# Order of the opening's weight loads, ScalarE's rounding of two weights, one weight scaled a batch earlier, and idle matrix products in three stretches

## The chip, the core and the metric

The kernel runs on one core of one Trainium2 chip. The metric is the time of one execution on the device in microseconds (us), as the median of several runs. The engines are TensorE (PE, matrix products), VectorE (DVE), ScalarE (ACT), GpSimd (POOL) and SyncE (SP, which here only issues transfers). TensorE's clock is granted at one of two levels, 2.4 GHz (shown as 1.00) and 1.2 GHz (0.50).

## What is computed

Two transformer layers over a batch of B = 32 items with T = 112 rows of D = 256 numbers, and a context of S = 375 rows for each item. All in float32, with four blocks in a row:

```
x = x + cross_attention_0(layernorm(x), ctx)     # 16 heads of 64, Wq Wk Wv: 256 -> 1024, Wo back, + bo
x = x + ffn_0(layernorm(x))                      # rows quantised to 8 bits, weights to -1, 0, 1; depthwise conv of 3 taps, silu
x = x + cross_attention_1(layernorm(x), ctx)     # 16 heads of 16, rms norm of q and k, rotation
x = x + ffn_1(layernorm(x))                      # one uint8 scale for ALL activations, int8 scale per weight row, relu
```

The weights of ffn_0 are quantised as `clip(round(w * scale), -1, 1)` with `scale = 1 / clip(mean(|w|), 1e-5)`. The weights of ffn_1 are quantised row by row: `scale = max(|w|) / 127`, `round(w / scale)`. The activations of ffn_1 share one scale, `max(x) / 255`, over the whole batch, so ffn_1 can begin only when all 32 items have passed the third block; its hidden layer has a second such scale.

## The kernel before, in words

Each engine runs a program of its own, written out by hand; the engines meet only at semaphores (`wait_ge`, `then_inc`). There is no planner: the order of the lines is the order on each engine. A helper `link` makes a DVE instruction wait for the one before it.

**Precision.** A product that has to be near exact is made from split operands: `hi` is the operand rounded to the format `F32R`, `lo` is what is left, and three products hi·lo, lo·hi and hi·hi are summed (`exact3`, six matmuls since the depth is 2 x 128). ACT makes `hi` by a copy, DVE makes `lo` of a weight by a subtraction, POOL makes `lo` of the context (`ctx_lo`, L1493 to 1496).

**Opening** (L262 to 301 on SP, L647 to 671 on PE, L917 to 933 on ACT, L1297 to 1341 on DVE, L1561 to 1566 on POOL). SP loads ident, the first context (`craw`), the first x, wk0 into `stage[0]`, wv0 into `stage[1]`, eight small constants and wq0. `stage` has two rooms of 128 x 2048 numbers, and each next weight waits until its room is free: wkv1 after wk0's lo (semaphore `w_lo` 1), f0w1 after wv0's lo, f0w2 after wkv1's lo, and wo0 after f0w1 is quantised (`w_quant` 1). DVE clears some tiles and marks that with `zeros_ready`. ACT rounds wk0, then the context; DVE and POOL subtract. PE then makes the keys of item 0 (`k0_proj`, eight pieces), the values (`v0_proj`, six), the queries (`q0_proj`, two), and goes into the attention. DVE makes the ternary weights in `ternary(n, part)` (L1098 to 1116): a sum of absolute values (part 0), mean and reciprocal behind PE's product with ones (`weight_sum`, part 1), then four passes over 2048 numbers (parts 2 to 4: scale and clip above, clip below and add ROUND, subtract and clip, clip and cast). For f0w1 these stand before the attention of the opening, for f0w2 inside it, at i = 2, 4 and 6.

**Attention** (`attention(part, b)` on PE L496, ACT L819, DVE L1135, POOL L1502) works through pairs of heads, i = 0 to 7 in the opening and in the closing, 0 to 15 in a middle batch, where layer 0 of the next item and layer 1 of this one are mixed. A pair goes: scores (PE, L410), maxima (DVE, L1048), two exps (ACT, L808), reciprocal of the sums (DVE, L1056), scaling (POOL, L1508), turning (PE, L434 or L424), copies of the turned rows (half by ACT, L768, half by DVE, L1039 or L1035), products with the values (PE, L446 for layer 0, L461 for layer 1). Scores run two pairs ahead. PE's turn of pair i waits for ACT's and DVE's copies of pair i - 1. Behind the last pairs stand the keys and values of layer 1 (`kv1_proj`), which DVE squares and sums (`k1_squares`) and POOL rotates, and the product with Wo (`wo0_product`), whose second half and the residual belong to the next batch.

**Loop.** For b = 0 to 30 every engine runs `rest(b, False)` and `attention(MIDDLE, b)`. `rest` finishes layer 0 of item b (residual x1, quantisation xq, ffn_0 with its convolution, x2) and the query of layer 1, and PE fills its waits with the projections of item b + 1.

**Last batch** (L616 to 639 and the branches with `last_batch`). `rest(31, True)` has no next item, so the fills fall away. DVE there also prepares the weights of ffn_1: `scales(0, 0)` (largest of each row, L1177 to 1180), `scales(0, 1)` (division, L1182) and `scales(0, 2)` (rounding, L1185) stand between `oT_lo` and x1 (L1194 to 1200), `scales(1, 0)` ahead of x2 (L1257), `scales(1, 1)` behind it. `attention(CLOSING, 31)` follows.

**Tail** (PE L680 to 762). The weights are turned, the global scale is found with two small products (L692 and L694, `spread`), the hidden layer is made once for its maximum (`hidden`, L701, with `largest` on DVE, L1412), a second `spread` follows (L726, L728), then the hidden layer is made again (`hidden_again`), passed through ACT's relu (L986), rounded by DVE and multiplied with the second weight (`second`, L743); POOL adds the residual (L1582, L1587) and SP stores.

## Time and profile before

| | us |
|---|---|
| median of 3 runs | 2382.2 (2381.74 to 2383.67) |
| the profiled execution, its own time | 2380.98 |
| its span, first to last instruction | 2379.2 |
| mean granted TensorE clock | 0.989 |

| engine | busy us | share of the span |
|---|---|---|
| PE | 2294.8 | 96% |
| DVE | 1663.5 | 70% |
| POOL | 1628.8 | 68% |
| ACT | 1510.5 | 63% |

A line of the timeline gives the start in us, the duration in us, the engine, the line of the kernel, the operation, what it writes and reads, the shape and a count; where neighbours are merged, the duration runs over all of them. In brackets stands how long the engine had stood idle before it, and who ended that. Matmuls overlap, so the duration of a few of them is longer than the distance of their starts. A wait is put down to the semaphore that came last by the profile.

### The profile page before, as it was taken

The numbers are of one execution on the slowest core, as the hardware profiler recorded it, in microseconds if no ns is written. First come the engines' busy times: TensorE is split into PE (matmuls) and PEld (weight loads), VectorE is DVE, ScalarE is ACT, GpSimd is POOL, SyncE is SP. The second block draws the span as 40 slices with busy tenths as digits, with TensorE's granted clock in tenths as the row PEclk, the third lists the DMA queues.
The fourth block names the chain that finished last, engine by engine and source line by source line (L and its number), as shares of the span: only waits on it lengthen the run. The fifth ranks groups of instructions, "written<-read, shape, count | busy, mean of one in ns | idle before, by whom it ended". The sixth has DMA issues, their size and how long they took to land.

```text
span 2379.2 us, 61055 instructions
## 1 busy us (share of the span) xinstructions
PE 2294.8 (96%) x20320; PEld 1774.9 (75%) x20320; DVE 1663.5 (70%) x4061; ACT 1510.5 (63%) x4306; POOL 1628.8 (68%) x1830
## 2 busy tenths in 40 slices
PE   6999999999999999999999999999999999999578
PEld 5777777777787777777777777787777777777336
DVE  6766666776767667766666776767667666666785
ACT  4666666666666666666666666666666666666356
POOL 3676776676768767676776676767767676776507
PEclk9999999999999999999999999999999999999689
DMA  4000000000000000000000000000000000001202
GB/s 146 10 11 10 10 8 10 2 10 10 10 10 8 10 2 10 10 10 10 10 8 9 3 10 10 10 10 8 10 2 10 10 10 10 10 2 38 54 10 63
DMA packets 31197, 37.04 MB, mean 16 GB/s; under 512 B 3284, under 2 KB 29636, under 8 KB 31172
## 3 DMA queue, kind: packets, MB, share of 16 engines
q1 hardware_dynamic: 31172, 36.71, 5.3%
q8 instruction: 15, 0.25, 0.0%
q14 instruction: 10, 0.08, 0.0%
HBM read 29.36 MB, written 7.34 MB: 15 GB/s over the span
## 4 chain that ended last, share of the span: by engine, by line
PE 92%; DVE 3%; POOL 2%; issue 2%; ACT 1%; DMA 0%; POOLq 0%; SPq 0%; ACTq 0%; DVEq 0%
PE ps L349 25%; PE ps L410 17%; PE pt L434 11%; PE pa L446 7%; PE pt L424 5%; PE ps L393 5%; PE pa L486 4%; PE pa L461 4%; PE pa L349 2%; PE pt L349 2%; PE pa L584 1%; PE pt L609 1%; PE ps L474 1%; DVE th L1412 1%; PE pa L624 1%
## 5 line engine op out<-in xcount | busy, mean ns | idle before, releaser
L1048 DVE TENSOR_REDUCE nmx<-ps 112x2 f32<-112x750 f32 x512 | 480.1, 938 | 197.0 <-PE ps L410 190.9
L1508 POOL TENSOR_TENSOR prob<-prob,rinv 112x375 f32<-112x375 f32 x512 | 404.9, 812 | 197.6 <-DVE rinv L1056 197.6
L1508 POOL TENSOR_TENSOR f1w_room<-f1w_room,rinv 112x375 f32<-112x375 f32 x512 | 405.4, 817 | 64.3 <-DVE rinv L1056 64.3
L768 ACT ACTIVATE room<-ps 128x375 f32<-128x375 f32 (+2 forms) x480 | 227.8, 488 | 303.9 <-PE ps L349 303.9
L768 ACT ACTIVATE probT<-pt 125x336 f32<-125x336 f32 (+1 forms) x512 | 242.6, 474 | 195.8 <-PE pt L424 142.1
L808 ACT ACTIVATE prob<-ps,nmx 112x375 f32<-112x375 f32 x512 | 289.8, 580 | 65.7 <-DVE nmx L1048 65.7
L808 ACT ACTIVATE f1w_room<-ps,nmx 112x375 f32<-112x375 f32 x512 | 291.2, 587 | 2.4 <-DVE nmx L1048 2.3
L1533 POOL TENSOR_TENSOR krs<-krs,nhalf 125x48 f32<-125x48 f32 x32 | 256.9, 8030 | 0.0
L410 PE MATMUL ps<-kT,q 64*112 64x375 f32 x1024 | 234.6, 517 | 1.0 <-ACT prob L808 1.0
L410 PE MATMUL ps<-room,q 64*112 64x375 f32 x1024 | 230.7, 515 | 3.0 <-ACT prob L808 1.9
L1039 DVE COPY probT<-pt 125x336 f32<-125x336 f32 x322 | 162.7, 505 | 96.2 <-PE pt L434 96.2
L446 PE MATMUL pa<-probT,room 125*64 125x112 f32 x3072 | 182.5, 264 | 0.0
L434 PEld LDWEIGHTS pt<-ident,prob 112*125 112x125 f32 x966 | 118.1, 188 | 84.0 <-issue 75.1
L434 PEld LDWEIGHTS pt<-ident,f1w_room 112*125 112x125 f32 x966 | 121.2, 188 | 67.2 <-issue 44.0
L446 PEld LDWEIGHTS pa<-probT,room 125*64 125x64 f32 x3072 | 148.2, 136 | 19.6
L349 PE MATMUL ps<-cT_hi,wk_lo 128*128 128x376 f32 x512 | 136.7, 348 | 15.4 <-POOL cT_lo L1495 15.4
L434 PE MATMUL pt<-ident,prob 112*125 112x112 f32 x966 | 144.1, 285 | 4.3 <-ACT probT L768 1.1
L1224 DVE SCALAR_TENSOR_TENSOR z<-hp,convw,z 128x112 f32<-128x112 f32 x512 | 140.6, 330 | 8.8
L1490 POOL TENSOR_TENSOR st<-st,lneps 112x1 f32<-112x1 f32 x96 | 20.6, 215 | 178.6 <-DVE st L1020 178.6
L349 PE MATMUL ps<-cT_lo,wk_hi 128*128 128x376 f32 x512 | 140.9, 347 | 1.5 <-POOL cT_lo L1495 1.5
L434 PE MATMUL pt<-ident,f1w_room 112*125 112x112 f32 x966 | 137.1, 278 | 4.3 <-DVE probT L1035 1.0
L349 PE MATMUL ps<-cT_hi,wk_hi 128*128 128x376 f32 x512 | 130.2, 335 | 0.0
(270 smaller groups left out, 5326.0 us busy)
## 6 DMA issues: line engine op xcount, KB each, us to landing
craw<-in_ctx SPq DMA_DIRECT2D x32, 375.0 KB, 3.1
xin<-in_x SPq DMA_DIRECT2D x32, 112.0 KB, 2.0
x_rows<-x SPq DMA_DIRECT2D x32, 112.0 KB, 1.9
out<-probT SPq DMA_DIRECT2D x16, 224.0 KB, 2.3
room<-x_rows SPq DMA_DIRECT2D x1, 2576.0 KB, 12.8
w<-in_f1w SPq DMA_DIRECT2D x2, 1024.0 KB, 6.7
stage<-in_wk SPq DMA_DIRECT2D x1, 1024.0 KB, 7.3
stage<-in_wv SPq DMA_DIRECT2D x1, 1024.0 KB, 9.8
```

The source lines that it names most:

```text
L349: last = pe.matmul(dst, left(l, c), right(r, c), start=(n == 0), stop=(n == len(TERMS) - 1))
L393: last = pe.matmul(ps[:, g + 1, j * T:(j + 1) * T], wq0[:, c, (HT * g + j) * P:(HT * g + j + 1) * P], xn0T[:, c, :], start=(c == 0), stop= ...
L410: last = pe.matmul(ps[0:T, 2 * (i % 2) + n, 0:S], q, k, start=True, stop=True)
L434: last = pe.transpose(pt[0:SK, n, t * T:(t + 1) * T], prob(i, n)[:, t * SK:(t + 1) * SK], ident[0:T, 0:T])
L446: last = pe.matmul(pa[r:r + DH0, p // HT, (p % HT) * T:(p % HT + 1) * T], v0[0:SK, t, h * DH0:(h + 1) * DH0], probT[:, 2 * (i % 4) + n, t, :],
L768: return act.activation(dst, src, ACT.Copy)
L808: ins = act.activation(prob(i, n), ps[0:T, 2 * (i % 2) + n, 0:S], ACT.Exp, bias=nmx[:, g:g + 1], accum_out=rsum[:, g:g + 1])
L1039: dve.tensor_copy(probT[:, 2 * (i % 4) + 1, :, :], pt[0:SK, 1, 0:KT * T].rearrange("p (k t) -> p k t", k=KT))\
L1048: top = dve.tensor_reduce(nmx[:, g:g + 2], ps[0:T, 2 * (i % 2):2 * (i % 2) + 2, 0:S], AX_X, ALU.max, negate=True)
L1224: ins = dve.scalar_tensor_tensor(z[:, j, :], hp[:, j, tap:tap + T], convw[:, j, tap:tap + 1], z[:, j, :], ALU.mult, ALU.add)
L1508: pool.tensor_tensor(prob(i, n), prob(i, n), rinv[:, g:g + 1].to_broadcast([T, S]), ALU.mult).then_inc(s["normed"], 1)
L1533: step.link(pool, pool.tensor_tensor(krs[:, 2, :], krs[:, 1, :], nhalf[0:SK, :], ALU.pow))
```

## The change

1. **Loads.** wk0 is loaded in two halves of 512 columns, the context between them, ident and x behind. ACT and DVE make its hi and lo half by half, PE starts its first four pieces on the first half. Every later count of `w_lo` and `w_hi` is one higher.
2. **Clearing.** DVE clears only the pad column of cT, and POOL clears v1 before its first wait. `whole` holds +ROUND and -ROUND for ACT.
3. **Ternary weights.** Per weight DVE keeps the sum, mean and reciprocal, and one pass that clips. ACT does the scaling with rounding (`weight_round`) and the shift back with the cast (`weight_shift`). For f0w1 the round stands between v0's fourth and fifth copy and the shift at i = 1 of the attention; for f0w2 sum, mean and clip stand at i = 1, 2 and 4 on DVE, round and shift at i = 3 and 5 on ACT, the product with ones at i = 2 on PE. The rounding of wo0 moves from i = 5 to 6 on ACT, its subtraction from behind the last pair to i = 7 on DVE. PE's waits move: `late_in` and `w_lo` to the projection of layer 1's keys, v0's last copy to i = 3, `w_quant` 1 away (DVE waits for `w_quant` 2 behind the last pair).
4. **Last weight.** `scales(0, 0)` and `scales(0, 1)` move from `rest(31, True)` into the end of `attention(MIDDLE, 30)`; DVE's loop ends one batch earlier and batch 30 is written out.
5. **Idle products.** `idle_products(n, bank)` multiplies the same operands of 128 and 376 columns n times into a bank nobody reads: 12 behind the first two scores of the opening, 14, 28, 10, 8 and 12 in `rest(31, True)`, 14 before and 14 behind the first pass over the hidden layer.

The core of the diff:

```diff
@@ -96,6 +96,7 @@
+        whole = sb("whole", [P, 2])
@@ -216,9 +217,12 @@
+        stage_half, hi_half, lo_half = ([v[:, :, n * INNER // 2:(n + 1) * INNER // 2] for n in range(2)]
+                                        for v in (stage[0].rearrange("p (c n) -> p c n", c=DC), wk0[0], wk0[1]))
@@ -270,10 +274,12 @@
+            wk0_half = [A["wk0"].rearrange("(c p) n -> p c n", p=P)[:, :, n * INNER // 2:(n + 1) * INNER // 2] for n in range(2)]
+            load_w(stage_half[0], wk0_half[0], "wk0_in")
+            load_ctx(0)
+            load_w(stage_half[1], wk0_half[1], "wk0b_in")
             load_w(ident[:], A["ident"], "ident_ready")
-            load_ctx(0)
             load_x(0)
-            load_w(stage[0], A["wk0"].rearrange("(c p) n -> p c n", p=P), "wk0_in")
@@ -281,15 +287,15 @@
-            sp.wait_ge(s["w_lo"], 1)
+            sp.wait_ge(s["w_lo"], 2)
...
-            sp.wait_ge(s["w_lo"], 2)
+            sp.wait_ge(s["w_lo"], 3)
...
-            sp.wait_ge(s["w_lo"], 3)
+            sp.wait_ge(s["w_lo"], 4)
@@ -518,6 +524,10 @@
+                    if part == OPENING and i == 2:
+                        weight_sum(1)
+                    if part == OPENING and i == 3:
+                        pe.wait_ge(s["v0_sb"], 6)
@@ -527,6 +537,9 @@
                             pe.wait_ge(s["exped"], at(count - 1, part, b))
+                            if part == OPENING:
+                                pe.wait_ge(s["w_lo"], 4)
+                                pe.wait_ge(s["late_in"], 64)
                         kv1_proj(k, i - (count - 2))
@@ -558,6 +571,9 @@
+                else:
+                    idle_products(14, ps[:, 1, 0:SE])
@@ -578,6 +594,8 @@
+                else:
+                    idle_products(28, ps[:, 1, 0:SE])
@@ -589,6 +607,8 @@
+                else:
+                    idle_products(10, ps[:, 1, 0:SE])
@@ -612,6 +632,8 @@
+                else:
+                    idle_products(8, ps[:, 1, 0:SE])
@@ -630,6 +652,7 @@
+                    idle_products(12, ps[:, 1, 0:SE])
@@ -638,36 +661,39 @@
+            def idle_products(count, bank):
+
+                for _ in range(count):
+                    pe.matmul(bank, wv0[0][:, 0, 0:P], cT[0][:, 0, :], start=True, stop=True)
...
-                pe.matmul(pt[:, 0, n:n + 1], ones[:], wmean[:, n:n + 1], start=True, stop=True)\
+                pe.matmul(pa[:, 1, n:n + 1], ones[:], wmean[:, n:n + 1], start=True, stop=True)\
...
-            pe.wait_ge(s["ident_ready"], 16)
...
-            k0_proj(0, range(IC), False)
+            k0_proj(0, range(HT), False)
...
+            k0_proj(0, range(HT, IC), False)
+            pe.wait_ge(s["w_lo"], 3)
...
-            pe.wait_ge(s["zeros_ready"], 1)
-            weight_sum(0)
+            pe.wait_ge(s["ident_ready"], 16)
             x0_transpose(0)
             v0_proj(0, [2])
...
             q0_proj(0, 1)
+            weight_sum(0)
             v0_proj(0, [4, 5])
-            weight_sum(1)
-            pe.wait_ge(s["late_in"], 64)
-            pe.wait_ge(s["w_quant"], 1)
-            pe.wait_ge(s["w_lo"], 3)
             pe.wait_ge(s["k0_sb"], IC)
             pe.wait_ge(s["q0_sb"], 2)
-            pe.wait_ge(s["v0_sb"], 6)
+            pe.wait_ge(s["v0_sb"], 5)
             for i in range(AHEAD):
                 scores(i, OPENING, 0)
+            idle_products(12, pt[:, 0, 0:SE])
             attention(OPENING, 0)
             pe.wait_ge(s["w_quant"], 2)
@@ -693,6 +719,7 @@
+            idle_products(14, ps[:, 1, 0:SE])
@@ -722,6 +749,8 @@
+            pe.wait_ge(s["xq3T_sb"], NCH + 1)
+            idle_products(14, pa[:, 1, 0:SE])
@@ -809,6 +838,12 @@
+            def weight_shift(n):
+
+                act.wait_ge(s["w_clip"], n + 1)
+                act.activation(flat((f0w1, f0w2)[n], BF16), stage[1 - n], ACT.Identity, bias=whole[:, 1:2])\
+                    .then_inc(s["w_quant"], 1)
@@ -820,7 +855,11 @@
-                    if part == OPENING and i == 5:
+                    if part == OPENING and i in (1, 5):
+                        weight_shift(i // 5)
+                    if part == OPENING and i == 3:
+                        weight_round(1)
+                    if part == OPENING and i == 6:
@@ -914,20 +953,29 @@
+            def weight_round(n):
...
+                act.wait_ge(s["w_scale"], n + 1)
+                act.activation(stage[1 - n], stage[1 - n], ACT.Identity, bias=whole[:, 0:1],
+                               scale=wmean[:, (3, 6)[n]:(3, 6)[n] + 1]).then_inc(s["w_round"], 1)
...
+            act.wait_ge(s["wk0_in"], 16)
+            copy(hi_half[0], stage_half[0]).then_inc(s["w_hi"], 1)
+            act.wait_ge(s["zeros_ready"], 1)
+            ctx_hi(0)
+            act.wait_ge(s["wk0b_in"], 16)
+            copy(hi_half[1], stage_half[1]).then_inc(s["w_hi"], 1)
+            act.wait_ge(s["wv0_in"], 16)
+            copy(flat(wv0[0], F32R), stage[1]).then_inc(s["w_hi"], 1)
...
             x0_copy(0)
-            v0_copy(0, [2, 3, 4, 5])
+            v0_copy(0, [2, 3])
+            weight_round(0)
+            v0_copy(0, [4, 5])
@@ -1104,16 +1152,12 @@
-                    link(dve.tensor_scalar(wmean[:, m:m + 1], pt[:, 0, n:n + 1], 1.0 / (F * D), 1e-5, ALU.mult,
...
+                    dve.reciprocal(wmean[:, r:r + 1], wmean[:, m:m + 1]).then_inc(s["w_scale"], 1)
+                else:
+                    dve.wait_ge(s["w_round"], n + 1)
+                    dve.tensor_scalar(w, w, ROUND - 1.0, ROUND + 1.0, ALU.max, ALU.min).then_inc(s["w_clip"], 1)
@@ -1132,12 +1176,32 @@
+            def attention(part, b, last_middle=False):
...
-                    if part == OPENING and i in (2, 4, 6):
-                        ternary(1, i // 2 + 1)
+                    if part == OPENING and i == count - 1:
+                        dve.wait_ge(s["wo0_hi"], 1)
+                        dve.tensor_tensor(wo0_lo[:], stage[1].rearrange("p (c n) -> p c n", c=IC), wo0_hi[:].bitcast(F32),
+                                              ALU.subtract).then_inc(s["wo0_lo"], 1)
+                    if part == OPENING and i in (1, 2, 4):
+                        ternary(1, (1, 2, 4).index(i))
@@ -1151,14 +1215,16 @@
-                    dve.wait_ge(s["wo0_hi"], 1)
...
+                    dve.wait_ge(s["w_quant"], 2)
...
                     values_lo(k, 0)
                     k1_squares(k, 0)
+                    if last_middle:
+                        scales(0, 0)
                     k1_squares(k, 1)
                 turned(count - 1, part, b)
+                if last_middle:
+                    scales(0, 1)
@@ -1193,8 +1243,7 @@
-                    for part in range(3):
-                        scales(0, part)
+                    scales(0, 2)
@@ -1294,57 +1343,57 @@
-            dve.memset(ones[:], 1.0)
-            dve.memset(cT[0][:].bitcast(F32), 0.0)
-            dve.memset(cT[1][:].bitcast(F32), 0.0)
-            dve.memset(hp[:], 0.0)
...
+            dve.memset(cT[0][:, :, S:SE].bitcast(F32), 0.0)
+            dve.memset(cT[1][:, :, S:SE].bitcast(F32), 0.0)
+            dve.memset(nhalf[:], -0.5)
+            dve.memset(lneps[:], LN_EPS).then_inc(s["xq3T_sb"], 1)
...
-            dve.memset(v1[:], 0.0)
...
+            dve.memset(whole[:, 0:1], ROUND)
+            dve.memset(whole[:, 1:2], -ROUND)
+            dve.memset(ones[:], 1.0)
+            dve.memset(hp[:], 0.0).then_inc(s["zeros_ready"], 1)
             dve.wait_ge(s["zeros_ready"], 1)
-            dve.wait_ge(s["w_hi"], 1)
-            dve.tensor_tensor(flat(wk0[1], F32R), stage[0], flat(wk0[0]), ALU.subtract).then_inc(s["w_lo"], 1)
-            dve.wait_ge(s["w_hi"], 2)
+            for n in range(2):
+                dve.wait_ge(s["w_hi"], n + 1)
+                dve.tensor_tensor(lo_half[n], stage_half[n], hi_half[n].bitcast(F32), ALU.subtract).then_inc(s["w_lo"], 1)
+            dve.wait_ge(s["w_hi"], 3)
...
             normalise(xn0[:], xin[:], 0, 0).then_inc(s["xn0_ready"], 1)
+            dve.wait_ge(s["w_hi"], 4)
+            dve.tensor_tensor(flat(wkv1[1], F32R), stage[0][:, 0:DC * 2 * D], flat(wkv1[0]), ALU.subtract)\
+                .then_inc(s["w_lo"], 1)
...
             link(dve.tensor_copy(identb[:], ident[:]))
...
-            dve.wait_ge(s["w_hi"], 3)
-            dve.tensor_tensor(flat(wkv1[1], F32R), stage[0][:, 0:DC * 2 * D], flat(wkv1[0]), ALU.subtract)\
-                .then_inc(s["w_lo"], 1)
             ternary(0, 0)
+            q0_copy(0, 0)
+            q0_copy(0, 1)
             ternary(0, 1)
-            for part in range(2, 5):
-                ternary(0, part)
-            q0_copy(0, 0)
-            ternary(1, 0)
-            q0_copy(0, 1)
-            ternary(1, 1)
+            ternary(0, 2)
...
-            with dve.Fori(0, B - 1) as b:
+            with dve.Fori(0, B - 2) as b:
                 step.begin(b)
                 rest(b, False)
                 attention(MIDDLE, b)
                 step.end()
-            step.begin(B - 1)
+            step.begin(B - 2)
+            rest(B - 2, False)
+            attention(MIDDLE, B - 2, True)
             rest(B - 1, True)
             attention(CLOSING, B - 1)
@@ -1558,6 +1607,7 @@
+            pool.memset(v1[:], 0.0)
```

`scales` itself is unchanged and only stands ahead of DVE's `attention` now.

## Rows read from the trace of the kernel before

**Rows 1.** Busy time by stretch, the whole loop: stretch, length, engines, PEclk, DMA, GB/s.

```profile
68.40:2199.40 2131.00, 2120.23 (x19101) 1653.65 (x19100) 1494.88 (x3751) 1385.79 (x4061) 1522.86 (x1741) 1.00 0.03 10
```

**Rows 2.** Timeline of the opening's start: the first weight, the context, the first product.

```profile
9.47 1.91 ACT L768 ACTIVATE wk_hi<-stage 128x2048 fp32r<-128x2048 f32 x1 [7.45 <-DMA stage<-in_wk]
...
12.25 3.03 POOL L1495 TENSOR_TENSOR cT_lo<-craw,cT_hi 128x750 fp32r<-128x750 f32 x1 [11.80 <-ACT cT_hi L768]
...
15.42 0.96 PE L349 MATMUL ps<-cT_hi,wk_lo 128*128 128x376 f32 x2 [15.42 <-POOL cT_lo L1495]
```

**Rows 3.** Timeline of DVE at the change from batch 30 to batch 31.

```profile
2193.38 0.42 DVE L1085 TENSOR_REDUCE krs<-room 125x16 f32<-125x256 f32 x1 [2.50 <-ACT v L768]
...
2196.31 0.42 DVE L1085 TENSOR_REDUCE krs<-room 125x16 f32<-125x256 f32 x1 [0.48 <-ACT v L768]
...
2198.58 0.63 DVE L1133 COPY mr<-st 112x2 f32 x1
...
2200.03 2.28 DVE L1177 TENSOR_REDUCE t<-w 128x8 f32<-128x2048 f32 x1
...
2202.79 2.29 DVE L1182 TENSOR_TENSOR w<-w,t 128x2048 f32<-128x2048 f32 x1
2205.11 1.23 DVE L1185 TENSOR_SCALAR last_weights<-w 128x2048 bf16<-128x2048 f32 x1
2206.26 0.41 DVE L1200 TENSOR_TENSOR x<-pa,xbo 112x256 f32<-112x256 f32 x1
```

**Rows 4.** Timeline of the opening's attention, first scores to the loop's first batch.

```profile
39.75 1.52 PE L410 MATMUL ps<-room,q 64*112 64x375 f32 x8 [0.66 <-ACT room L768]
...
46.63 1.81 DVE L1111 TENSOR_SCALAR stage<-stage,wmean 128x2048 f32<-128x2048 f32 x1
...
60.95 2.28 DVE L1155 TENSOR_TENSOR wo_lo<-stage,wo_hi 128x2048 fp32r<-128x2048 f32 x1
...
64.62 0.81 PE L434 MATMUL pt<-ident,f1w_room 112*125 112x112 f32 x6
...
68.85 1.64 POOL L1495 TENSOR_TENSOR cT_lo<-craw,cT_hi 128x750 fp32r<-128x750 f32 x1
...
70.54 0.61 PE L349 MATMUL ps<-cT_lo,wk_hi 128*128 128x376 f32 x2 [1.51 <-POOL cT_lo L1495]
```

**Rows 5.** Timeline of POOL in the last batch, behind x2.

```profile
2228.03 2.56 POOL L1490 TENSOR_TENSOR st<-st,lneps 112x1 f32<-112x1 f32 x1 [2.17 <-DVE st L1020]
```

**Rows 6.** Busy time by stretch, the first key products (columns as rows 1).

```profile
16.00:21.00 5.00, 5.00 (x18) 5.00 (x17) 3.95 (x8) 0.96 (x2) 1.45 (x3) 1.00 0.45 146
22.00:26.00 4.00, 4.00 (x25) 4.00 (x25) 1.92 (x2) 2.66 (x5) 0.00 (x0) 1.00 0.52 174
```

**Rows 7.** Busy time by stretch, PE's standstill in the last batch (columns as rows 1).

```profile
2201.00:2205.00 4.00, 0.00 (x0) 0.00 (x0) 3.90 (x4) 0.00 (x0) 0.00 (x0) 1.00 1.05 242
2206.00:2207.00 1.00, 0.00 (x0) 0.00 (x0) 0.97 (x3) 0.00 (x0) 0.00 (x0) 0.50 1.10 288
```

**Rows 8.** Timeline and one line's durations (min/median/max, ns), batch 0 and last batch.

```profile
77.49 0.96 PE L572 MATMUL pt<-xqT,f0w_q 128*128 128x112 bf16 x16
...
2210.84 1.70 PE L572 MATMUL pt<-xqT,f0w_q 128*128 128x112 bf16 x16
...
L584 PE MATMUL pa<-ident,th x256: 270/273/462, 84.7 to 2219.9; 128*112 128x128 f32 x128
...
2226.73 0.48 DVE L1259 SCALAR_TENSOR_TENSOR x<-pt,am,x 112x256 f32<-112x256 f32 x1 [0.85 <-PE pt L609]
```

**Rows 9.** Timeline of the tail, the first maximum and the first relu.

```profile
2273.06 1.09 DVE L1412 TENSOR_REDUCE th<-ps 128x2 f32<-128x896 f32 x1 [0.89 <-PE ps L701]
...
2315.70 2.77 ACT L986 ACTIVATE stage<-ps,t 128x448 f32<-128x448 f32 x4 [10.42 <-PE ps L701]
```

**Rows 10.** Busy time in the opening's attention, and ACT's table loads.

```profile
45.00:50.00 5.00, 3.68 (x31) 2.46 (x31) 4.76 (x8) 3.60 (x12) 4.53 (x5) 1.00 0.00 0
...
L768 ACT ACT_TABLE_LOAD x1 | 1.3, 1283 | 0.7 <-PEq L1640 0.7
```

83 lines of the change are left out of this document (32 added, 51 removed).

## The prediction

> **What bounds the kernel now.** I read the page first: TensorE (PE) is busy 96% of the span (the table above). The busy time by stretches says where not: over the 31 batches of the loop it is 2120 of 2131 us [rows 1]. Nothing there can be shortened by other engines, and the change leaves that code as it is. So everything is in three stretches whose sum is some 250 us: the opening (0 to 68 us), the last batch (2199.4 to 2261) and the tail (2261 to the end). In the timeline of the opening PE stands still until 15.42, behind the weight's load, ScalarE's (ACT's) rounding of weight and context, and GpSimd's (POOL's) remainder of the context [rows 2]. In the last batch there is no next batch to project, so every wait of PE is on the path; in its first one VectorE (DVE) scales a weight before it adds the residual [rows 3]. Times are against the profiled execution, 2380.98 us (span 2379.2 and 1.8 around it); the median 2382.2 stands 1.2 above, and I subtract from the median.
>
> **Opening, start.** Half of wk0 now comes first, then the context, then the other half, with ident and x behind. Before, wk0 was waited for until 9.47 behind three transfers [rows 2]. With 0.5 MB in front instead of 1.5 I put the first half at 5.5 us (4.5 to 7). DVE's memsets (big cT and v1 ones gone, v1's on POOL ahead of everything) end by then. ACT's copy of half a weight is some 1.0 us (half of 1.91 [rows 2]), the context copy some 0.8 (750 of 1024 elements): POOL can start near 7.7. POOL's subtraction took 3.03 us beside DVE's [rows 2] and 1.64 alone [rows 4]; I take 2.0, as only halves of 1.2 us run beside it. First product at 9.8 (8.5 to 12), 5.6 us earlier.
> A POOL operation that began 0.23 us before a DVE one with two inputs still lasted until that ended: 2.56 us [rows 5]. By the Trainium skill (SBUF — State Buffer, on the shared port pair) whichever starts first holds the pair and the other blocks; so the subtraction would need its 1.64 and the first product would come at 9.4. The row disagrees with it.
> The products then run at half speed for a while, as before: 18 began in 5 us between 16 and 21, 25 in 4 us between 22 and 26 [rows 6]: 0.28 against 0.16 each, 0.31 against 0.17 by the starts of neighbours. That ramp starts earlier with them, so little is lost. The waits on late_in, w_quant, w_lo and v0's last copy in front of the first scores go or sink into the opening attention: 0.9 us, of which 0.6 is real. First scores: 39.75 becomes about 33.4.
>
> **Opening, attention.** Three ACT passes over 2048 elements are added among the exps: two weight_shift, one weight_round, 1.91 each by the copy of that size [rows 2], 5.7 in all; the first round stands before v0's fifth copy, where ACT waits for PE anyway. DVE loses four passes of about 1.8 and gets a sum of 2.3 (the time of any pass of its that reads 2048 elements at full precision from two places or into a sum [rows 3, 4]) and a clip of 1.8: 3.1 less [rows 4]. ACT's passes stand in front of the copies of turned probabilities that PE's next turn waits for, and the sum of the second weight (PE waits for it at i = 2, DVE for PE) costs 1.5. I walked the eight pairs through the four queues with these durations. A pair's turn starts when the later of both copies of the pair before is done. Turn 1 comes at 43.0, as DVE makes the sum (2.3) ahead of maximum 3 and its copy; turn 2 at 46.3 (product with ones, mean, reciprocal, round at 46.9 to 48.7 behind exp 4); turn 3 at 49.2 (ACT's round in front of its copy of turn 2); turn 4 at 52.2; turn 5 at 55.2 (shift in front of the copy of turn 4, 52.8 to 54.6); turn 6 at 59.1 (wo_hi and oT in front of the copy of turn 5, 56.3 to 58.6); behind it two projections of 1.4 and turn 7. That is 3.0 us per pair, where DVE's full queue gave 2.5 before. From first scores to the last turn 24.9 us (39.75 to 64.62) become 30.4. So the last turn comes at 63.8, 0.8 earlier; 6.3 us of start have melted to that. But wo_lo (2.28 [rows 4]) now stands in front of turn 6 instead of in front of the k1 sums, so POOL starts its rotation and the next cT_lo 3 us earlier, and PE's idle of 1.51 us before 70.54 [rows 4] goes. 12 idle products at 0.17 are 2.05; exp 0 follows the first maximum, so scores(2) come 3.3 us after the first scores, 1.8 of them busy, and 0.3 is lost, included. SP's load of wo0 waits for the first weight_shift, 41.6 instead of 35.1, and ACT reads it at 56: covered by 14 us of which a transfer of that size takes some 6 to 7 (wk0 had 9.47 with half a MB ahead of it). **Sum of the opening: -3.0** (0 to -5.5).
>
> **Last batch, DVE.** scales(0, 0) moves between the sums of k1 0 and 1 of the batch before, scales(0, 1) behind the last turned copy. The first (2200.03 to 2202.79, 2.76) falls into DVE's wait there of 2.50 and makes the next sum 0.3 late for POOL, which has slack until 2207. The second (2.29 and 0.03) delays the rest of that queue, from k1's last sum over x3 to oT_lo: 0.48 of it covered by a wait, and I estimate 0.8 given back, since the peeled iteration writes mx3 and mr at a constant index and not at a register's (mr's copy of two elements took 0.63; others that small take 0.2), so oT_lo and the last product come 1.0 later. x1 then follows the 1.23 pass at 2202.2 instead of 2206.26 [rows 3]. **-4.1** (-3.3 to -4.7). What is late next: nothing else, PE's product ends at 2201.8. SP's store of x3 shifts 2 us; rows are needed 60 us later.
>
> **Last batch, idle products.** The granted clock was 1.00 (2.4 GHz) to 2205 and 0.50 (1.2 GHz) in 2206 to 2207, after PE had done nothing since 2201 [rows 7]. An idle product is 0.16 to 0.17 us at 2.4 GHz. 14 take 2.4 of 3.9 us; 28 take 4.8 of 6; 10 take 1.7 of 2.6 less a turn; 8 take 1.4 of about 2: none in the way if the clock stays. What full speed gives, in the rows of batch 0 against the last: the 16 products of L572 take 0.96 us instead of 1.70; hp waits for half of them and for rb's product, 0.7 together; L584's products last 0.27 us instead of 0.46, 0.5 to the first four [rows 8]; the transposes and f0w2 products save 2 us more, but scales(1, 0) holds DVE until 2225.9 while x2 came at 2226.73 after a wait of 0.85 for PE [rows 8]: 0.7. Sum **-1.9** (0 to -2.2). Behind x2 POOL waits for DVE's pass [rows 5] whatever PE does. The 12 end 5 us before the closing scores with one short transpose between, so these start at 1.2 GHz as before: 0 (to -1.5).
>
> **Tail.** 14 products after the weight copies end at 2267.8; the transposes come at 2269.2 and hidden products at 2271.3. The first maximum waited for four products at half speed [rows 9]; held, it comes 1.3 earlier, lost again in the gap, 0.4: I take **-0.9**. The other 14 fill 2.4 of 3.1 us before the second spread: ACT's first relu waited for PE [rows 9], four products 0.19 apart instead of 0.37: **-1.0** (-0.6 to -1.3).
>
> **Sum:** -3.0 - 4.1 - 1.9 - 0.9 - 1.0 = -10.9: 2371.3 (profiled 2370.1).
>
> **Rivals.** A, the opening gives nothing: ACT, 3.60 of 5 us busy in 45 to 50 [rows 10], becomes the bound and the 5.7 us eat all of it. For: each pass stands before a copy that PE waits for. Against: DVE, at 4.76 of 5, was the fuller one [rows 10] and loses 3. Time 2382.2 - 7.9 = 2374.3.
> B, everything holds better, opening -5 and the clock through the closing scores: 2367.5.
> C, the idle products run at half speed, 0.31 each, and stand in the way: 28 are 8.7 us in 5.7 (+3.0), the others +3.5, no clock gain: -7.1 + 6.5, 2381.6. Against: in the opening dense products brought the clock back within the first pieces, and PE is not allowed to stand as long as before [rows 6, 7].
> D, ACT's Identity among Exp passes costs a table load of 1.28 each way, six of them, 7.7: 2379.0. Against: the loop mixes Identity, Exp and Tanh, and the execution has one load, at its start [rows 10]. By the Trainium skill (ScalarE: Activation LUTs, What ACT_TABLE_LOAD costs) only a switch to another set pays; the trace agrees with its one load.
> E, slower: the steady loop gets longer. DVE enters it with other offsets and leaves it one batch earlier, and with PE at 99% any new wait there is paid 30 times: from 0.52 us per batch it outweighs the gain and the 0.2%; at 0.7 us 2392. Against: no instruction of the loop changes.
>
> **Chances.** Forecast 0.60, B 0.10, A 0.20, C 0.05, D 0.02, E 0.03. A measurement can tell 0.2%, 4.8 us. Faster 0.90 (forecast, A, B), within 0.07 (C, D), slower 0.03. Range: from B with the low bounds, 2366.0, to A with the clock gains halved, 2376.5.
>
> **What would show it.** First k0 product near 9.8; first scores near 33.4; in the opening attention ACT nearly full and turned copies late behind its passes; the loop's first cT_lo products near 67.5. x1 4.1 us closer to the last oT_lo. Granted clock 1.00 from there to the q1 transposes; 0.50 at the closing scores. Wrong it would be if the loop's length per batch moved, if idle products ended after their releaser, or if turn 7 stayed behind 66.

## The result, and the profile after

Each kernel has its median over several executions. The interval belongs to the ratio to the kernel before on the same chip.

| | kernel before | kernel after |
|---|---|---|
| median, us (4 runs each) | 2381.97 (2380.60 to 2383.67) | 2368.85 (2366.34 to 2369.41) |
| the profiled execution, its own time | 2380.98 | 2369.06 |
| its span | 2379.2 | 2367.1 |
| mean granted TensorE clock | 0.989 | 0.994 |

The ratio is 0.9943, 95% interval 0.9927 to 0.9959: 13.1 us faster by the medians, 12.1 us by the two profiled spans. The forecast was 2371.3 us, range 2366.0 to 2376.5.

The head of the page of the kernel after, with each engine's busy time:

```profile
span 2367.1 us, 61209 instructions
PE 2312.3 (98%) x20432; PEld 1794.0 (76%) x20432; DVE 1650.0 (70%) x4057; ACT 1517.9 (64%) x4311; POOL 1627.7 (69%) x1831
```

PE is busier than before by 17.5 us in a shorter span; that is the idle products, and it says nothing of the gain. For that I cut both spans at four places that both have. The first two cuts are the addition of x1 in batch 0 and in batch 31 (x1 is the residual that closes the first block of an item); these are its rows in the kernel before and in the kernel after (shortest, median and longest duration in ns, first and last start in us):

```profile
L1200 DVE TENSOR_TENSOR x<-pa,xbo x32: 414/425/426, 72.6 to 2206.3; 112x256 f32<-112x256 f32 x32
```

```profile
L1249 DVE TENSOR_TENSOR x<-pa,xbo x32: 416/424/425, 69.8 to 2198.3; 112x256 f32<-112x256 f32 x32
```

The other cuts are the product with wo1 that closes layer 1 (2259.94 and 2250.12) and the transpose for the second global scale (2312.66 and 2301.70).

| stretch, us | before | after | difference | forecast |
|---|---|---|---|---|
| start to batch 0's x1 (opening) | 72.6 | 69.8 | -2.8 | -3.0 |
| batch 0's x1 to batch 31's x1 (loop, DVE's move) | 2133.7 | 2128.5 | -5.2 | -4.1 |
| batch 31's x1 to wo1's product (last batch) | 53.7 | 51.8 | -1.9 | -1.9 |
| wo1's product to the second scale (tail) | 52.7 | 51.6 | -1.1 | -0.9 |
| the second scale to the end (tail) | 66.5 | 65.4 | -1.1 | -1.0 |

**Opening.** The timeline of the kernel after at its start, against [rows 2]:

```profile
4.75 1.06 ACT L797 ACTIVATE wk_hi<-stage 128x1024 fp32r<-128x1024 f32 x1 [2.73 <-DMA stage<-in_wk]
...
5.91 1.23 DVE L1365 TENSOR_TENSOR wk_lo<-stage,wk_hi 128x1024 fp32r<-128x1024 f32 x1 [2.64 <-ACT wk_hi L797]
6.84 1.80 POOL L1544 TENSOR_TENSOR cT_lo<-craw,cT_hi 128x750 fp32r<-128x750 f32 x1 [4.72 <-ACT cT_hi L797]
...
8.33 1.39 DVE L1365 TENSOR_TENSOR wk_lo<-stage,wk_hi 128x1024 fp32r<-128x1024 f32 x1 [1.19 <-ACT wk_hi L797]
8.79 0.97 PE L355 MATMUL ps<-cT_hi,wk_lo 128*128 128x376 f32 x2 [8.79 <-POOL cT_lo L1544]
```

The first product came 6.6 us earlier, and it still waits for the context's remainder on POOL. The busy time by stretch then shows what no row of before showed (length; PE, PEld, DVE, ACT, POOL; granted clock; DMA, GB/s):

```profile
40.00:42.00 2.00, 0.60 (x4) 0.00 (x0) 1.99 (x4) 2.00 (x3) 0.48 (x2) 0.93 0.01 4
42.00:44.00 2.00, 1.91 (x15) 1.83 (x15) 0.00 (x0) 1.32 (x5) 1.24 (x2) 0.50 0.36 101
...
46.00:48.00 2.00, 2.00 (x16) 1.80 (x17) 1.31 (x3) 2.00 (x4) 2.00 (x4) 0.50 0.88 299
48.00:50.00 2.00, 2.00 (x28) 1.60 (x24) 1.23 (x1) 2.00 (x6) 0.62 (x1) 0.87 0.04 8
```

PE stood for most of 40 to 42 us, and the clock then was granted at its lower level (1.2 GHz) until about 48.5. "PE busy 2.00" in the third row is 16 products in 2 us, where the next row has 28: the same work drawn out. The timeline of the attention, against [rows 4]:

```profile
32.83 1.52 PE L416 MATMUL ps<-room,q 64*112 64x375 f32 x8 [0.65 <-ACT room L797]
...
42.09 1.51 PE L430 MATMUL pt<-ident,prob 48*125 48x48 f32 x12
...
52.23 2.01 ACT L844 ACTIVATE f0w_q<-stage,whole 128x2048 bf16<-128x2048 f32 x1
...
54.72 0.88 PE L440 MATMUL pt<-ident,prob 112*125 112x112 f32 x6 [1.16 <-ACT probT L797]
...
58.41 0.88 PE L440 MATMUL pt<-ident,f1w_room 112*125 112x112 f32 x6 [1.40 <-ACT probT L797]
...
63.42 0.81 PE L440 MATMUL pt<-ident,f1w_room 112*125 112x112 f32 x6
...
67.72 0.61 PE L355 MATMUL ps<-cT_lo,wk_hi 128*128 128x376 f32 x2
```

Two turns wait for ACT's copy of the turned rows: the one at 54.72 behind the shift of the second weight (52.23 to 54.24), the one at 58.41 behind the rounding of wo0 (1.95 us from 55.54), a pass that the kernel before had, too. The last turn is 1.2 us earlier than before, and the product with cT_lo waits no longer.

**DVE between batch 30 and 31**, against [rows 3]:

```profile
2187.00 2.27 DVE L1185 TENSOR_REDUCE t<-w 128x8 f32<-128x2048 f32 x1
...
2191.95 2.28 DVE L1190 TENSOR_TENSOR w<-w,t 128x2048 f32<-128x2048 f32 x1
...
2196.33 0.17 DVE L1177 COPY mr<-st 112x2 f32<-112x2 f32 x1
2196.53 0.62 DVE L1128 TENSOR_TENSOR oT_lo<-pa,oT 128x448 fp32r<-128x448 f32 x1
...
2197.16 1.22 DVE L1193 TENSOR_SCALAR last_weights<-w 128x2048 bf16<-128x2048 f32 x1
2198.29 0.42 DVE L1249 TENSOR_TENSOR x<-pa,xbo 112x256 f32<-112x256 f32 x1
```

**Last batch.** PE's timeline from there on, against [rows 8]; L667 is the idle product:

```profile
2197.78 2.57 PE L667 MATMUL ps<-cT_hi,wv_hi 128*128 128x376 f32 x14
2201.89 0.27 PE L579 MATMUL pt<-identb,xq 112*128 112x112 bf16 x2 [1.55 <-DVE xq L1144]
...
2202.89 1.70 PE L588 MATMUL pt<-xqT,f0w_q 128*128 128x112 bf16 x16
2204.36 5.68 PE L667 MATMUL ps<-cT_hi,wv_hi 128*128 128x376 f32 x28
2210.36 1.38 PE L602 MATMUL pa<-ident,th 128*112 128x128 f32 x8 [0.32 <-DVE th L1283]
```

The 14 left a gap of 1.55 us (2200.34 to 2201.89), and just behind it, from 2202.3 to 2205.7, the clock was granted at its lower level: the 16 products took 1.70 us as before. It came back while the 28 ran, and they ended 0.32 us ahead of what they stood in front of. The second half of the weight for layer 1 then sits ahead of x2 on DVE with no wait, as forecast:

```profile
2214.71 2.29 DVE L1185 TENSOR_REDUCE t<-w 128x2 f32<-128x2048 f32 x1
...
2217.44 0.48 DVE L1308 SCALAR_TENSOR_TENSOR x<-pt,am,x 112x256 f32<-112x256 f32 x1
```

**Tail**, against [rows 9]:

```profile
2262.48 2.09 DVE L1461 TENSOR_REDUCE th<-ps 128x2 f32<-128x896 f32 x2
```

```profile
2303.68 5.03 ACT L1034 ACTIVATE stage<-ps,t 128x448 f32<-128x448 f32 x8 [9.37 <-PE ps L728]
```

The first maximum starts 10.58 us earlier than before and the first relu 12.02, where wo1's product was 9.82 earlier.

### The profile page after: what moved, and what is told of

Read it like the earlier page. It is cut to its first block, busy times and chain, and to the rows that moved or that the text cites. A ratio compares the mean times of both kernels' runs of the same rounds, so it can differ in the third digit from the quotient of the medians.

```text
span 2367.1 us, 61209 instructions
## 1 busy us (share of the span) xinstructions
PE 2312.3 (98%) x20432; PEld 1794.0 (76%) x20432; DVE 1650.0 (70%) x4057; ACT 1517.9 (64%) x4311; POOL 1627.7 (69%) x1831
## 4 chain that ended last, share of the span: by engine, by line
PE 92%; DVE 3%; issue 2%; POOL 2%; ACT 1%; DMA 0%; POOLq 0%; ACTq 0%; DVEq 0%
PE ps L355 26%; PE ps L416 17%; PE pt L440 11%; PE pa L452 7%; PE pt L430 5%; PE ps L399 5%; PE pa L492 4%; PE pa L467 4%; PE pa L355 2%; PE pt L355 2%; PE pa L602 1%; DVE th L1461 1%; PE pt L629 1%; PE pa L646 1%; PE ps L480 1%
```

## The experiments

All carry the change except where the edit says otherwise. After each median stands its range; the kernel before had 2380.93 us beside the first four, 2380.89 beside the next four, 2382.39 beside the last four. These groups ran on chips of their own, so a median is best read against its own kernel before. By the ratios, experiments 4, 5, 6 and 9 (0.9943 to 0.9946) cannot be told from the change itself (0.9943): what they show, they show in the stretches of one profiled execution each. x2, used below, is the residual that closes ffn_0. The last section of the experiments puts the stretches of all of them side by side.

**1. No idle products.**

```diff
-                    idle_products(28, ps[:, 1, 0:SE])
+                    pass
```

and so for all other calls.

> The changed kernel with all six calls of the idle products left out; everything else is as changed. Theory P (parts add up, each where the two traces differ): the idle products are worth 0.3 to 0.5 us in front of the GELU reduce, 0.8 us to x2, 0.5 us in the closing attention, 1.1 us to the first hidden maximum and 1.1 us at the second global scale, and nothing in the opening; so the time is 2368.85 + 4.0 = 2372.9 us, batch 31's x1 starts within 0.3 us of 2198.3, and x2 follows x1 by 20.4 us (the kernel before: 20.47) and not by 19.15. Rival N (the last batch shifts earlier by DVE's work alone, and TensorE's clock comes back by itself): the time stays within 1 us of 2368.9 us. Rival O (the idle products in the opening hold the clock there): batch 0's x1 starts 1 us or more later than 69.8.

Measured: 2372.64 (2371.91 to 2377.53, 6 runs), ratio to before 0.9968 (0.9956 to 0.9980); 3.8 us over the changed kernel's median, 4.8 us if each is taken against its own kernel before. Busy time by stretch (columns as above):

```profile
2200.00:2216.00 16.00, 6.07 (x40) 5.09 (x41) 13.03 (x38) 6.43 (x15) 13.16 (x4) 0.54 0.59 139
```

x1 to x2 took 20.5 us, as before. P holds and N falls. O falls as well: with no idle products x1 came at 68.7, earlier than 69.8, though the clock was down there too (0.50 from 38 to 46 us). From the first scores to x1 it took 36.4 us, and 36.9 to 37.6 us in the four executions that have the same opening with its 12 idle products (the kernel after, experiments 2, 5 and 12). The 12 of the opening gave nothing.

**2. The opening alone.** Scaling and idle products behind the opening as before.

> The kernel with the changed opening alone (its idle products too); the last weight's scaling stands behind batch 30's loop turn again, and there are no idle products in the last batch or the tail. Theory P: batch 0's x1 at 69.8 as in the changed kernel (2.8 us ahead of the kernel before), and the end earlier by those 2.8 us: 2382.0 - 2.8 = 2379.2 us, plus or minus the scatter of the loop, which I put at 1 us. Rival L (the further 1.0 us that the changed kernel gains evenly over the 30 turns of the loop comes from the opening, say from where it leaves a buffer or a queue): the loop turn, (batch 30's x1 less batch 0's) / 30, is 68.617 us as in the changed kernel and not 68.653, and the time is 2378.2 us. Rival S (the 6.9 us that the first scores come earlier reach the end once nothing else is in the way): 2375 us.

Measured: 2377.02 (2374.93 to 2381.89, 11 runs), ratio 0.9986 (0.9977 to 0.9994): 3.9 us under before. x1 at 69.3, a loop turn of 68.63 us. P holds by x1. The median lies between P (2378.1 on this chip's kernel before) and S (2374.0); S falls, since its 6.9 us are outside the interval (1.4 to 5.5 us) and x1 shows 3.3. L is answered with the table below. The profiled execution was one of the two longest of the eleven (2381.16). Its last batch shows where its time went:

```profile
2201.00:2250.00 49.00, 26.70 (x133) 17.39 (x135) 31.89 (x74) 17.74 (x50) 29.69 (x19) 0.50 0.18 44
```

The clock did not come back for the whole last batch, whose code is that of the kernel before. There it was at 0.50 from 2206.0 to 2226.4 and from 2229.8 to 2246.9, and at full level between these and behind them. From x1 to wo1's product it took 57.9 us here and 53.7 there.

**3. The kernel before with DVE's move alone.**

```diff
+                    if last_middle:
+                        scales(0, 0)
                     k1_squares(k, 1)
                 turned(count - 1, part, b)
+                if last_middle:
+                    scales(0, 1)
```

> The kernel before with the scaling of the last weight alone moved into the last drain of layer 0 (DVE's loop is then 30 turns and one peeled). Theory P: batch 0's x1 at 72.6 as before, batch 31's x1 4.1 us earlier (about 2202.1), the time 2382.0 - 4.1 = 2377.9 us. Rival L' (the loop's 1.0 us comes from the peel): the loop turn is 68.617 us, batch 31's x1 at 2201.1, the time 2376.9 us. Rival W (the 2.3 us multiplication beside the keys' squares on POOL delays batch 31's drain): x1 no earlier than 2204, the time 2380 us.

Measured: 2377.91 (2373.47 to 2383.69, 12 runs), ratio 0.9988 (0.9980 to 0.9997): 3.0 us under before. From batch 0's to batch 31's x1 it took 2130.7 us instead of 2133.7. The 30 turns of the loop were 1.1 us longer in this execution, so the last turn alone says it better: from batch 30's x1 to batch 31's it took 69.96 us, before 74.07, 4.1 us less, as forecast. Its opening was late by itself (x1 at 76.5: first product at 16.68, clock 0.57 from 46 to 58), which no part of the edit touches; so the old opening can lose the clock, too. W falls by the stretch, L' by its loop turn, 68.69.

**4. The opening's attention held at full clock.**

```diff
+                    if part == OPENING and i == 2:
+                        pe.wait_ge(s["v0_sb"], 6)
+                        idle_products(5, pa[:, 0, 0:SE])
                     if i + AHEAD < count:
                         scores(i + AHEAD, part, b)
+                    if part == OPENING and i == 2:
+                        idle_products(9, pa[:, 0, 0:SE])
```

> The changed kernel with 5 more idle products ahead of the fifth scores of the opening attention and 9 behind them, where TensorE stood idle for 0.8 and 1.5 us at 39.0 to 42.1 us and the granted clock then was at its lower level to 48.5 us. Theory C (the low clock holds the opening attention up): the granted clock stays 1.0 from 42 to 49 us, turn 1 is issued in 0.75 us instead of 1.5, the values in 1.0 instead of 2.0, and the loop's first work comes 1.0 us earlier: batch 0's x1 at 68.8, the time 2367.9 us. Rival A (ScalarE's rounding passes set the pace of the opening attention, and the low clock lies beside them): x1 at 69.8 within 0.2 us, the time 2368.9 us. Rival H (14 idle products are not enough work and the clock falls all the same): lower level somewhere in 42 to 49 us, x1 at 69.8.

Measured: 2367.78 (2366.33 to 2369.18, 5 runs), ratio 0.9946 (0.9933 to 0.9959). The clock read 1.00 throughout the opening; turn 1 took 0.88 us in place of 1.51. Its first scores came at 32.39, 0.44 earlier by scatter, and x1 at 68.3: from first scores to x1 35.9 instead of 37.0 us. Experiment 9, held as well, has 35.9 again, and the executions that are not held, with the same opening, have 36.9 to 37.6. So the low clock cost 1.0 us in the kernel after and up to 1.7 in others, as theory C has it. The waits of turns 5 and 6 for ACT stayed, 1.21 and 1.39 us, which is A's share.

**5. Last batch and tail held.**

```diff
-                    idle_products(14, ps[:, 1, 0:SE])
+                    idle_products(22, ps[:, 1, 0:SE])
...
-                    idle_products(12, ps[:, 1, 0:SE])
+                    idle_products(26, ps[:, 1, 0:SE])
                     query_turn(b, 0)
+                    idle_products(8, ps[:, 1, 0:SE])
...
+            idle_products(6, pa[:, 1, 0:SE])
             pe.wait_ge(s["g_used"], 1)
...
-            idle_products(14, ps[:, 1, 0:SE])
+            idle_products(18, ps[:, 1, 0:SE])
```

> The changed kernel with more idle products where the granted clock still fell: 22 instead of 14 ahead of batch 31's input transposes (TensorE stood idle there for 1.55 us and the clock was at its lower level from about 2202.8 to 2205), 26 instead of 12 behind the last queries' product and 8 more between its two turns (idle for 3.02 and 1.69 us, the closing scores then at the lower level), and in the tail 6 new ones ahead of the first global transpose and 18 instead of 14 ahead of the first hidden products. Theory C (a stretch filled with products keeps the clock, and each gap let it fall): hp 0.7 us earlier after x1, the eight first closing products 1.5 us instead of 2.85 and the closing attention 1.5 us shorter, the first hidden maximum 0.4 us earlier: 2368.85 - 2.6 = 2366.3 us. Rival W (the longer rows stand in the way of TensorE's next product): no term gains, the time 2369 to 2371 us. Rival D (DVE and ScalarE set the closing attention's start, so only its clock and not its end moves): 2367.8 us.

Measured: 2367.81 (2365.12 to 2371.66, 6 runs), ratio 0.9943 (0.9930 to 0.9956). The clock stood at full level through last batch and tail, and hp's products ran at it:

```profile
2195.00:2325.00 130.00, 107.67 (x783) 72.59 (x783) 99.31 (x214) 68.21 (x138) 49.77 (x39) 1.00 0.14 36
```

```profile
2198.89 3.94 PE L668 MATMUL ps<-cT_hi,wv_hi 128*128 128x376 f32 x22
2203.00 0.27 PE L579 MATMUL pt<-identb,xq 112*128 112x112 bf16 x2 [0.17 <-DVE xq L1146]
...
2203.75 0.95 PE L588 MATMUL pt<-xqT,f0w_q 128*128 128x112 bf16 x16
```

x1 to x2 is 18.5 us instead of 19.1, x1 to wo1's product 49.5 instead of 51.8: 2.3 us. The filled gap is not the only way to the 0.6: the 14 idle products with the same gap of 1.55 us stand in six kernels, and in four of them (the kernel after, experiments 4, 7 and 8) the clock fell behind it, in two (6 and 12) it did not, and x1 to x2 was 18.5 in 6, too. With the 22 it fell there in none of four (5, 9, 10, 11). The tail gained nothing (117.0 us from wo1's product to the end, as in the changed kernel); the first maximum's 0.35 us is lost again in DVE's pass over the weights. C holds for the batch, not for the tail's 0.4. The median moved by 1.0 only, within its spread.

**6. The second weight's last pass on DVE.**

```diff
-                    if part == OPENING and i in (1, 5):
-                        weight_shift(i // 5)
+                    if part == OPENING and i == 1:
+                        weight_shift(0)
...
+                else:
+                    dve.tensor_scalar(flat(f0w2, BF16), w, ROUND, None, ALU.subtract).then_inc(s["w_quant"], 1)
```

> The changed kernel with the second weight's last pass (ScalarE, 2.0 us, 50.8 to 52.8 us in the run with the clock held) given to DVE at the seventh turn of the opening attention, where DVE waited 2.77 us for ScalarE. Theory A (ScalarE's passes set the end of the opening attention: turns 5 and 6 of the changed kernel waited 1.16 and 1.40 us for its copies of probT): turn 5 comes 1.2 us earlier, batch 0's x1 1.0 to 2.0 us earlier, at 68.3, the time 2367.3 us. Rival Q (the chain goes over to the last output weight's split, two passes later on ScalarE and DVE): x1 not over 0.5 us earlier, 2368.5 us.

Measured: 2368.56 (2366.80 to 2371.24, 5 runs), ratio 0.9944 (0.9931 to 0.9958). x1 at 70.1. Inconclusive: turns 5 and 6 waited no longer, but this execution had the clock down longer than the changed kernel (43.8 to 57.4 us against 41.7 to 48.5):

```profile
42.00:56.00 14.00, 13.70 (x95) 10.24 (x93) 9.11 (x17) 10.14 (x24) 6.98 (x9) 0.56 0.36 113
```

**7. Rounding of both weights on DVE, four passes each.**

```diff
-                    dve.wait_ge(s["w_round"], n + 1)
-                    dve.tensor_scalar(w, w, ROUND - 1.0, ROUND + 1.0, ALU.max, ALU.min).then_inc(s["w_clip"], 1)
+                elif part == 2:
+                    link(dve.tensor_scalar(w, w, wmean[:, r:r + 1], 2.0, ALU.mult, ALU.min))
...
-                    if part == OPENING and i in (1, 2, 4):
+                    if part == OPENING and i in (1, 2, 4, 5, 6):
```

The other passes are those of the kernel before, and ACT's rounding and shifts are gone.

> The changed kernel with the rounding of both layer-0 weights back on DVE in four passes of 1.23 us each (scale, round, clip twice), at the places of the changed order; ScalarE is freed of its two passes of 2.1 and two of 2.0 us, and the keys' weight is still split in halves. Theory P (ScalarE's rounding carries a part of the opening's 2.8 us): DVE's first row maximum comes 1.1 us later (34.9 instead of 33.8), the second weight adds 3.7 us to DVE in turns 4 to 6, and batch 0's x1 comes 1 to 2.5 us later than 69.8; the time 2370.5 us. Rival A (ScalarE is the fuller engine of the opening attention, the swap is even): x1 within 0.5 us of 69.8 or earlier, the time 2368.9 us.

Measured: 2371.61 (2369.80 to 2373.01, 5 runs), ratio 0.9955 (0.9942 to 0.9968). x1 at 71.6, 1.8 us later, which is what P says. But the clock was down for 13.6 us here (44.9 to 58.5) and for 6.8 in the changed kernel, so this execution alone does not decide it; experiment 11 does.

**8. The old order of loads.**

```diff
+            load_w(ident[:], A["ident"], "ident_ready")
+            load_ctx(0)
+            load_x(0)
             load_w(stage_half[0], wk0_half[0], "wk0_in")
-            load_ctx(0)
             load_w(stage_half[1], wk0_half[1], "wk0b_in")
-            load_w(ident[:], A["ident"], "ident_ready")
-            load_x(0)
```

> The changed kernel with the loads in the order of before: identity, context, input rows, and then the two halves of the keys' weight. Theory K (the first product waits for the context's low part on POOL, and that for ScalarE behind the first half of the weight): 551 KB now stand ahead of the first half, at 330 to 400 GB/s some 1.5 us, so the first product is at 10.3 instead of 8.8 us and batch 0's x1 at 71.0 instead of 69.8 at most; the time 2370 us. Rival G (the start is given back at the opening attention, as 4 of the 6.9 us were): first product at 10.3, x1 within 0.4 us of 69.8, 2369 us.

Measured: 2373.28 (2370.80 to 2377.13, 7 runs), ratio 0.9966 (0.9954 to 0.9978). The first half was there at 7.5 us instead of 4.75:

```profile
7.51 1.06 ACT L797 ACTIVATE wk_hi<-stage 128x1024 fp32r<-128x1024 f32 x1 [5.49 <-DMA stage<-in_wk]
...
11.55 0.96 PE L355 MATMUL ps<-cT_hi,wk_lo 128*128 128x376 f32 x2 [11.55 <-POOL cT_lo L1544]
```

First product 2.8 us later (1.5 expected), first scores 1.7 later, x1 at 71.9, 2.1 later. So K, with a larger delay than its sum had, and what reaches the first scores reaches x1 as well while ACT's queue behind it stays the same. G falls.

**9. Everything held.** Edits 4 and 5 together.

> The changed kernel with the added idle products of both earlier runs: the opening attention (5 and 9), the last batch (22, 26 and 8) and the tail (6 and 18). The granted clock should read 1.0 from the first scores to batch 31 and through the closing. Theory C: the two gains add: batch 0's x1 at 68.3 (as with the opening held), batch 31's x1 to the end of the span 166.5 us (as with the last batch held, 168.8 in the changed kernel): the time is 2368.85 - 1.2 - 2.3 = 2365.3 us, with a spread of under 3 us over its runs. Rival N (the two gains were scatter): 2368 us.

Measured: 2367.86 (2366.84 to 2370.25, 5 runs), ratio 0.9944 (0.9931 to 0.9958). The opening kept its gain (x1 at 67.9, 35.9 us behind the first scores). The last batch did not: 52.2 us from x1 to wo1's product instead of 49.5. The same products ran at the same places, with the same gaps, and the clock fell at 2230.8, behind the closing scores:

```profile
2226.48 1.52 PE L416 MATMUL ps<-kT,q 64*112 64x375 f32 x8
2229.65 0.89 PE L416 MATMUL ps<-kT,q 64*112 64x375 f32 x4 [1.66 <-ACT prob L844]
2230.76 1.60 PE L416 MATMUL ps<-kT,q 64*112 64x375 f32 x4 [0.22 <-ACT prob L844]
```

In experiment 5 the same gap of 1.66 us had no such consequence, nor in experiment 11. Set beside experiment 5 product by product, this execution keeps its distance from x1 up to 2230.8 and falls behind only while the clock is down. Neither theory: the opening's gain came again, the last batch's is there only where the clock stays up. That the open gap ahead of the second closing scores is what lets it fall is likely, not shown.

**10. Everything held, and the pass of experiment 6.** Edits 4, 5 and 6 together.

> The run above with the second weight's last pass on DVE at the seventh turn. With the clock held, the test of that pass is no longer mixed with where the clock falls (in the first test it lay at its lower level from 43 to 57 us, and x1 came at 70.1). Theory A (ScalarE's 2.0 us pass sets turns 5 and 6, which waited 1.21 and 1.39 us for its copies in the run with the opening held): batch 0's x1 at 66.9 to 67.3 instead of 68.3, the time 2364.2 us. Rival Q (the chain goes over to the last output weight's split, on ScalarE and DVE): x1 at 68.0 to 68.4, 2365.3 us.

Measured: 2364.51 (2364.33 to 2367.75, 5 runs), ratio 0.9927 (0.9913 to 0.9940), the fastest of all; the profiled execution was the slowest of the five, with the clock down from 2216.5 to 2219.9 and from 2230 to 2240. Four of the five are faster than all of experiment 9, on the same chip. With the clock held in the opening the pass shows its worth:

```profile
51.15 0.91 PE L440 MATMUL pt<-ident,prob 112*125 112x112 f32 x6
...
54.23 0.88 PE L440 MATMUL pt<-ident,f1w_room 112*125 112x112 f32 x6 [0.76 <-ACT probT L804]
```

Turn 5 waits for nothing, turn 6 for 0.76 us. x1 at 65.8, 34.3 us behind the first scores against 35.9: the pass on ACT cost 1.6 us. Theory A holds and Q falls; x1 is 1.1 us earlier than A's range, 0.5 of which is a start that came earlier than in experiment 9.

**11. Everything held, rounding on DVE.** Edits 4, 5 and 7, with

```diff
-            idle_products(12, pt[:, 0, 0:SE])
+            idle_products(20, pt[:, 0, 0:SE])
...
-                        idle_products(5, pa[:, 0, 0:SE])
+                        idle_products(2, pa[:, 0, 0:SE])
```

> The held kernel (opening, last batch, tail) with the rounding of both weights back on DVE, in four passes each; the idle products behind the first scores are 20 instead of 12 and those ahead of the fifth 2 instead of 5, to fit its gaps. Theory P: with the clock held the opening with ScalarE's rounding is 1.0 to 1.5 us shorter: x1 at 69.5 here against 68.3, the time 2366.5 us. Rival A (only the place where the clock fell made the first run with DVE's rounding 1.8 us later): x1 at 68.3 within 0.3 us.

Measured: 2368.97 (2367.24 to 2370.32, 5 runs), ratio 0.9945 (0.9931 to 0.9958). The clock was at full level from 30 us to the loop and x1 came at 69.8, 1.9 us behind experiment 9, with the first scores within 0.04 us of each other. This is P without the clock in between. It is more than the 1.0 to 1.5 expected; the second weight's four passes took 1.65 to 1.81 us each inside the attention, not 1.23. The median is 1.1 us over experiment 9's, within the scatter.

**12. Twice the idle products ahead of the transposes behind the activation.**

```diff
-                    idle_products(28, ps[:, 1, 0:SE])
+                    idle_products(56, ps[:, 1, 0:SE])
```

> The changed kernel with 56 instead of 28 idle products ahead of the transposes behind the GELU. Theory F (28 are free only because DVE's chain takes longer than they do; in the changed kernel they ended 0.32 us ahead of what they stood before): 28 more at 0.18 us, less 0.32 us, put all of the last batch behind them back by 4.7 us: batch 31's x1 to x2 23.8 us instead of 19.1, the time 2373.5 us. Rival H (the clock gives some back, since nothing later falls): 2371 us. Rival Z (idle products never delay anything): 2368.9 us.

Measured: 2373.41 (2369.94 to 2374.99, 5 runs), ratio 0.9962 (0.9949 to 0.9976).

```profile
2203.59 9.86 PE L667 MATMUL ps<-cT_hi,wv_hi 128*128 128x376 f32 x56
2213.28 1.03 PE L602 MATMUL pa<-ident,th 128*112 128x128 f32 x8
```

x1 to x2 took 21.8 us: 2.7 more than in the changed kernel, 3.3 more than in experiment 5, where the clock was at full level in front of them as here. F in kind, less in size: the row started 1.0 us sooner behind x1 and ran at the full clock from its first product, and both took from the 4.7.

**All stretches side by side**, us, one profiled execution each:

| kernel | to x1 of batch 0 | x1 to x1 | to wo1's product | to second scale | to the end |
|---|---|---|---|---|---|
| before | 72.6 | 2133.7 | 53.7 | 52.7 | 66.5 |
| 2 opening alone | 69.3 | 2132.8 | 57.9 | 52.9 | 66.5 |
| 3 move alone | 76.5 | 2130.7 | 53.6 | 52.7 | 66.5 |
| 1 no idle products | 68.7 | 2129.3 | 53.8 | 52.8 | 66.5 |
| after | 69.8 | 2128.5 | 51.8 | 51.6 | 65.4 |
| 4 opening held | 68.3 | 2128.8 | 51.8 | 51.6 | 65.5 |
| 5 last batch held | 70.0 | 2129.4 | 49.5 | 51.5 | 65.5 |
| 6 the pass moved | 70.1 | 2128.7 | 50.3 | 51.5 | 65.4 |
| 7 rounding on DVE | 71.6 | 2129.5 | 51.9 | 52.8 | 65.5 |
| 8 old load order | 71.9 | 2129.9 | 51.9 | 52.4 | 65.5 |
| 9 all held | 67.9 | 2128.9 | 52.2 | 51.5 | 65.5 |
| 10 all held, the pass moved | 65.8 | 2129.3 | 53.9 | 51.5 | 65.5 |
| 11 all held, rounding on DVE | 69.8 | 2129.0 | 49.5 | 51.9 | 65.5 |
| 12 twice the 28 | 69.4 | 2129.1 | 54.5 | 51.6 | 65.5 |

The second column answers L and L'. With DVE's move it lies between 2128.5 and 2130.7, without it at 2132.8 and 2133.7; the loop turn reads 68.62 to 68.69 us over all, with the granted clock 1.00 in every turn, and follows neither the opening nor the peel (batch 30 written out). The changed kernel had the shortest of them. The extra 1.0 us of its loop is scatter. The last turn, from batch 30's x1 to batch 31's, is free of it: 74.07 us before, 73.77 in experiment 2, and 69.95 to 69.99 in all twelve kernels with the move. The last column is 65.45 to 65.47 us in every kernel that has the tail's idle products.

## Why the prediction was right

**Opening, start.** Half a weight was there at 4.75 (5.5 forecast), its copy took 1.06 (1.0), POOL began at 6.84 (7.7) and took 1.80 (2.0). The first product came at 8.79 instead of 9.8, the first scores at 32.83 instead of 33.4. Of the 6.6 us of start, experiment 8 gives 2.8 to the order of the loads, of which 2.1 arrive at x1; the other 3.9 (halves, fewer memsets, the context ahead of the second half) were not taken apart. On the shared port pair: POOL's subtraction began 0.30 us before DVE's first half ended, and DVE's second began 0.31 before POOL's ended and took 1.39 instead of 1.23. POOL's 1.80 is between the 1.64 alone [rows 4] that I gave for the page and the 2.0 I took. By the Trainium skill (SBUF — State Buffer, on the shared port pair) the one that starts first holds the pair and the other waits: that fits these two rows to 0.15 us, 0.30 + 1.64 = 1.94 and 0.31 + 1.23 = 1.54, and still does not fit [rows 5].

**Opening, attention.** The walk through the queues gave turns at 43.0, 46.3, 49.2, 52.2, 55.2, 59.1 and 63.8; they came at 42.09, 45.58, 49.80, 51.38, 54.72, 58.41 and 63.42. 6.9 us of start became 2.8 at x1: from the first scores to x1 it took 36.95 us instead of 32.85. Of these 4.1 us experiment 10 gives 1.6 to one ACT pass in front of a copy that PE waits for, the reason given in the forecast, and experiment 4 gives 1.0 to the clock; the other 1.5 are not shown. That the rounding is better on ACT than on DVE all the same is experiment 11's, by 1.9 us. The sum was right, its parts less so. Written out, it has 0.8 for the last turn and 1.5 for PE's wait behind it, 2.3 in all, and no term for the other 0.7 of the 3.0; measured were 1.2 and 1.6. DVE's clip took 1.23 us, not 1.8. And the clock: I weighed it in the last batch and at the start, not in the opening's attention, where PE's two waits of 0.82 and 1.49 us let it fall. That cost 1.0 us (experiment 4), hidden in the sum by a start 0.6 us better than forecast and by DVE's shorter clips (ACT's passes were longer than the 1.91 forecast, 2.00 to 2.10). That the total came within 0.2 us is in part luck.

**DVE's move.** -4.1 forecast. Against the last turned copy of batch 30, which was 3.81 us earlier than before, x1 was 7.97 earlier: 4.16. The last turn of all kernels says the same: 74.07 became 69.95. The forecast's sign, "4.1 us closer to the last oT_lo", left out its own 1.0 for oT_lo: oT_lo came 0.9 later behind that copy, and x1 is 5.1 closer to it. The copy of mr took 0.17 instead of 0.63, but not because its index is a constant now. This is the line of all its copies in the kernel before (shortest, median, longest in ns):

```profile
L1133 DVE COPY mr<-st x32: 168/170/626, 139.0 to 2262.6; 112x2 f32 x31, 112x2 f32<-112x2 f32 x1
```

31 of them had a register's index, and all but one of the 32 took 0.17; the row of [rows 3] was the one late copy. So the reason for "0.8 given back" was misread from a single row. It came all the same, since an ordinary copy is as short. Experiment 2 writes batch 30 out without the move, and its last turn is 73.77: 0.3 us of the 4.1 go with the written-out batch or with that one late copy, and 3.8 are the move's own. Experiment 3 gives 3.0 for stretch and median, the means of the second column 4.0.

**Idle products, last batch.** -1.9 forecast, -1.9 measured, but by other terms. The step that failed is the one at hp, the products behind the quantised rows: its 0.7 did not come, because "14 take 2.4 of 3.9 us; none in the way if the clock stays" took for granted that it stays over the rest, 1.55 us. Experiment 5 got it with the gap filled (0.6), experiments 6 and 12 with the gap open. The terms of the transposes behind the activation (called GELU in the expectations; 0.45 for 0.5) and of x2 (0.9 for 0.7) came. The closing scores ran at 1.2 GHz as forecast, but the clock was back earlier behind them, 0.5 us for 0. Experiment 1 bears out the whole: -3.8 us for all idle products by bare medians, -4.8 with each against its own kernel before, -4.2 by the last three columns, -3.8 forecast.

**Tail.** -0.9 and -1.0 forecast, -1.1 and -1.1 measured. Both columns go back to 52.8 and 66.5 without idle products. The first of the two gains is not certain even with them: experiments 7 and 8 read 52.8 and 52.4. There the clock was down from 2263.5 and from 2264.2 for 3.4 us, under the first hidden products, whose first eight took 3.16 us in 7 and 1.69 in the kernel after.

**The rivals.** A (opening gives nothing) fell: -2.8 in the trace, -3.9 by medians alone. B (everything better, 2367.5) did not come in the change, though its time is only 1.4 us from the measured median: the opening gave 2.8, not 5, and the closing scores ran at the lower level. Experiment 10, at 2364.5, is beyond it. C (idle products in the way) fell in the change, where 0.32 us was left even with some at half speed, and is what experiment 12 shows when they are too many. D (table loads) fell: one load, at the start, as before. E (a longer loop) fell: 68.62 against 68.65 us per turn. The sum was -10.9, the traces say -12.1, of which 1.0 is the loop's scatter: without that scatter the sum met the traces to 0.2 us; the medians' -13.1 has an interval of 3.8 us on either side.

## What to carry to other kernels

Cost a moved pass by whose queue it stands in and which copy the bottleneck waits for behind it: one pass of 2.0 us on the wrong engine was worth 1.6 us here, and a start 6.9 us earlier, together with such passes, was worth 2.8. Read a duration from all executions of its line, not from one row. Idle products pay where they cover the whole of a gap and end before what they stand in front of; behind a gap of 1.55 us left open the clock fell in four kernels of six, and 28 products too many cost 2.7 us. Look at the granted clock of every stretch in which the busy engine waits, the opening's too, and read a small gain as a stretch between two landmarks, since medians of the same few runs scatter by more.

## What the runs showed that I had not expected

The clock is not a function of the program alone. With the same 14 idle products and the same gap of 1.55 us the 16 products behind it took 1.70 us in the kernel after and 0.95 in experiment 12; and the closing scores of experiments 5 and 9 differ in the same way. Times scatter with it: experiments 2 and 3 spread over 7.0 and 10.2 us in 11 and 12 runs, the changed kernel over 3.1 in 4, the kernels with more idle products over 2.9 to 6.5 in 5 or 6. The kernel before spread over 3.1 us in 4 runs and 7.0 in 24, so these spreads do not show that idle products narrow it.

Leads can vanish in such dips. Batch 31's x1 started at 2197.1, 2199.4, 2196.8 and 2195.1 us in experiments 4, 5, 9 and 10, and wo1's product at 2248.91, 2248.91, 2248.95 and 2248.93. The clock was down for none of that stretch in 5, for some 7 us in 9, and for some 14 in 4 and in 10. That the four agree to 0.04 us may be chance; it stays open.

The first products of the execution started 0.31 us apart while the row of the granted clock read 1.00. That is the distance that products of this width had in experiment 10 where the clock read 0.50 (2217.7 to 2219.9); at full level it is 0.17:

```profile
9.00:14.00 5.00, 5.00 (x17) 5.00 (x18) 2.16 (x2) 2.76 (x3) 0.00 (x0) 1.00 1.07 343
15.00:19.00 4.00, 4.00 (x25) 4.00 (x25) 2.95 (x8) 2.65 (x6) 1.47 (x3) 1.00 0.76 243
```

So the granted clock of a stretch does not tell the speed of these; the distance between starts does.
